# Attention stages of a two-layer model on one core: PV products, copies and routing moved in the order, rotary tables scaled by VectorE

## What is computed

```
xn = layernorm(x)
x  = x + attention8(xn)[pred_values] + moe16(xn)       # 8 heads of 64, causal; 16 experts, 4 chosen
xn = layernorm(x)
x  = x + attention16(xn) + transformer6(xn)            # 16 heads of 8, causal; 6 layers, window 32
# transformer6, in each layer:
q, k = l2norm(q) * q_scale, l2norm(k) * k_scale        # then the rotary product with cos and sin tables
x = attention_window32(...) @ Wo + x ;  x = gelu_ffn(layernorm(x)) + x
```

## Time and profile before

| | us |
|---|---|
| median of 3 runs | 4737.76 |
| lowest, highest | 4735.57, 4738.05 |
| profiled execution, own time | 4733.7 |
| its span | 4731.7 |
| PE busy | 4372.4 (92%) |
| DVE busy | 3262.6 (69%) |
| ACT busy | 2762.9 (58%) |
| POOL busy | 2215.5 (47%) |

### The profile page before, as it was taken

The page is one execution under the profiler, slowest core; times in us unless marked ns, Lnnn a source line. Parts: engine busy times, 40 slices in busy tenths (PEclk is TensorE's granted clock), DMA queues, the critical chain, the costliest instruction groups (busy, mean ns, idle before and its releaser), DMA issues. The chain is left out here.

```text
span 4731.7 us, 170782 instructions
## 1 busy us (share of the span) xinstructions
PE 4372.4 (92%) x67636; PEld 2558.3 (54%) x67636; DVE 3262.6 (69%) x5741; ACT 2762.9 (58%) x5481; POOL 2215.5 (47%) x2020
## 2 busy tenths in 40 slices
PE   7888988898699999999999999999999999999995
PEld 4445544554355555555555555555555555555553
DVE  4556555655377777777777777777777777777772
ACT  4544554455256666666666666666666666566663
POOL 0000000000176676666666666666666666666661
PEclk9999999999899999999999999999999999999997
DMA  1000000000021112211121111211112111221112
GB/s 37 8 6 8 8 3 8 5 8 4 19 63 41 47 46 60 56 44 47 44 65 51 44 48 43 69 48 47 47 54 56 47 47 48 59 51 47 47 47 63
DMA packets 144849, 187.88 MB, mean 40 GB/s; under 512 B 34151, under 2 KB 66298, under 8 KB 144250
## 3 DMA queue, kind: packets, MB, share of 16 engines
q1 hardware_dynamic: 144250, 178.39, 14.0%
HBM read 29.39 MB, written 4.19 MB: 7 GB/s over the span
## 5 line engine op out<-in xcount | busy, mean ns | idle before, releaser
L1343 POOL TENSOR_TENSOR cs<-cs 128x512 f32<-128x512 f32 x768 | 980.5, 1277 | 575.2 <-DVE cs L1654 570.1
L1470 PE MATMUL psum<-wqkv,xw 128*128 128x512 f32 x2304 | 1191.6, 609 | 31.3 <-POOL xw L1380 24.9
L1654 DVE TENSOR_TENSOR cs<-psum,rots 128x1024 f32<-128x1024 f32 x768 | 938.0, 1222 | 295.3 <-PE psum L1470 249.5
L1352 POOL TENSOR_TENSOR qk<-cs,rn 128x512 f32<-128x512 f32 x768 | 777.2, 1044 | 338.0 <-ACT rn L1536 282.6
L1552 ACT ACTIVATE sq<-psum 128x512 f32<-128x512 f32 x768 | 459.2, 598 | 654.0 <-DVE cs L1654 645.3
L1378 POOL MEMSET qTl<- 128x2048 f32 x1 | 1.8, 1805 | 1270.0 <-POOLq L498 1270.0
L1615 DVE TENSOR_REDUCE ss<-sq 128x8 f32<-128x512 f32 x768 | 519.9, 677 | 6.9
L1421 PEld LDWEIGHTS psum<-pT,vw 64*64 64x64 f32 x18624 | 400.0, 135 | 191.1 <-issue 190.9
L1475 PEld LDWEIGHTS psum<-ident,qk 128*128 128x128 f32 x3088 | 352.5, 141 | 265.9 <-issue 152.0
L1475 PE MATMUL psum<-ident,qk 128*128 128x128 f32 x3088 | 445.6, 278 | 49.0 <-DVE state L1688 31.5
L1470 PEld LDWEIGHTS psum<-wqkv,xw 128*128 128x128 f32 x2304 | 368.6, 190 | 195.2 <-issue 169.9
(11 more groups left out here) (205 smaller groups left out, 6927.4 us busy)
## 6 DMA issues: line engine op xcount, KB each, us to landing
vw<-vl SPq DMA_DIRECT2D x768, 128.0 KB, 2.4
vw<-vl SPq DMA_DIRECT2D x672, 64.0 KB, 2.0
wqkv<-in_wqkv SPq DMA_DIRECT2D x42, 256.0 KB, 4.0
wol<-in_wol SPq DMA_DIRECT2D x7, 512.0 KB, 4.0
w1l<-in_w1l SPq DMA_DIRECT2D x7, 341.0 KB
xin<-in_x SPq DMA_DIRECT2D x9, 256.0 KB, 2.9
xr<-in_x SPq DMA_DIRECT2D x8, 256.0 KB, 2.8
sums<-sumout SPq DMA_DIRECT2D x8, 256.0 KB, 2.3
```

The costliest lines, as they stand in the source:

```text
L1343: summed_rot.done(nc.gpsimd.tensor_tensor(own, own, halves(cs[:, t % 2, j, 1, :])[:, :, ::-1, :], ALU.add), at)
L1352: rotated.done(nc.gpsimd.tensor_tensor(qk[:, j, :].rearrange("p (h c) -> p h c", c=EL), cs[:, t % 2, j, 0, :].rearrange("p (h c) -> p h c" ...
L1470: last = nc.tensor.matmul(ps[:, :], xw[:, t * P:(t + 1) * P], wqkv[:, col:col + BANK], start=True, stop=True)
L1654: parts.done(V.tensor_tensor(cs[:, t % 2, j, :, :].rearrange("p i (h c) -> p i h c", c=EL), twice, by_head, ALU.mult), at)
```

## The change

1. `wide_heads`: `at` of unit n-2 now stands ahead of `as` of unit n. PE's transposes come ahead of the scores and DVE's copies ahead of the maxima.
2. `narrow_heads`: the first scores of the next rank come ahead of `bn`, the last two PV products and `oe` of a rank (`rest_of`) come behind the first scores of the next rank (of the last rank: behind `as.0`), and `bp.r.1` comes ahead of `bt.r.2`.
3. Routing: `gr` comes earlier; pieces 0 to 6 stand among the projections, pieces 7 to 12 behind every second unit of the wide heads. `h1.0` comes ahead of the last `ap`.
4. In the second stage DVE scales the rotary tables: once ahead of the loop, and then behind the last `qk` step of each layer's last sample. ACT, DVE and POOL have the 8 samples written out, as PE has.

```diff
 def wide_heads(extra):
     for n in range(UNITS0 + PV_LAG0):
+        if n - TURN_LAG0 in range(UNITS0):
+            out.append(("at", n - TURN_LAG0))
         if n < UNITS0:
             out.append(("as", n))
-        if n - TURN_LAG0 in range(UNITS0):
-            out.append(("at", n - TURN_LAG0))
...
-def narrow_heads(r, scores):
-    s = scores + [[]] * (T - 1 - len(scores))
-    return (s[0] + [("bt", r, 0)] + s[1] + [("bt", r, 1), ("bp", r, 0)] + s[2]
-            + [("bt", r, 2), ("bp", r, 1), ("bp", r, 2), ("bp", r, 3), ("oe", r)])
+def narrow_heads():
+    out = []
+    for r in range(RANKS):
+        first, second, third = [[("bs", r + 1, i)] if r + 1 < RANKS else [] for i in reversed(range(1, T))]
+        out += first
+        out += [("bn", 0)] if r == 0 else rest_of(r - 1)
+        out += [("bt", r, 0)] + second + [("bt", r, 1), ("bp", r, 0)] + third + [("bp", r, 1), ("bt", r, 2)]
+        out += [("bo", r - 1)] if r else []
+        out += [("bn", r + 1)] if r + 1 < RANKS else []
+    return out
+
+def rest_of(r):
+    return [("bp", r, 2), ("bp", r, 3), ("oe", r)]
...
-SPLIT = {n + 1: [("rt", n)] for n in range(ROUTE)}
+EARLY = 7
+SPLIT = {2 * n + 2: [("rt", EARLY + n)] for n in range(ROUTE - EARLY)}
+CLOSE = {UNITS0 + 1: [("h1", 0)]}
...
+LOOP = (PROJECTED[:2] + [("ln",)] + PROJECTED[2:4] + [("gr",)] + PROJECTED[4:5] + [("x1t",), ("rt", 0), ("rt", 1)] + PROJECTED[5:7]
+        + [("rt", 2), ("rt", 3), ("q1",), ("k1",), ("rt", 4)] + PROJECTED[7:8] + [("rt", 5), ("rt", 6), ("v1",)] + PROJECTED[8:9]
+        + [("bs", 0, 3)] + PROJECTED[9:10] + [("bs", 0, 2)] + PROJECTED[10:11] + [("bs", 0, 1)] + PROJECTED[11:] + narrow_heads()
+        + wide_heads({**SPLIT, **CLOSE, 0: rest_of(LAST_RANK), 1: [("bo", LAST_RANK)], 3: [("ot",)], 5: [("y1",)]}) + EXPERT)
...
             with pool.Fori(0, DEPTH) as l:
-                parts.wait_before(pool, l * B, pieces[-1])
-                for a in range(2):
-                    for b in (2 * a, 2 * a + 1):
-                        nc.gpsimd.tensor_tensor(
-                            rots[:, b, :, :], rot[:, b, :, :],
-                            qks[:, a, bass.ds(l, 1), :].to_broadcast([P, T, EL]), ALU.mult).then_inc(scaled, 1)
-                with pool.Fori(0, B) as s:
+                for s in range(B):
...
+            def scale_tables(l):
+                for a in range(2):
+                    for b in (2 * a, 2 * a + 1):
+                        V.tensor_tensor(rots[:, b, :, :], rot[:, b, :, :], qks[:, a, bass.ds(l, 1), :].to_broadcast([P, T, EL]),
+                                        ALU.mult).then_inc(scaled, 1)
...
+            dve.wait_ge(rot_loaded, 48)
+            scale_tables(0)
             with dve.Fori(0, DEPTH) as l:
-                with dve.Fori(0, B) as s:
+                for s in range(B):
                     it = l * B + s
-                    dve.wait_ge(scaled, l * 4 + 8)
+                    dve.wait_ge(scaled, l * 4 + 4)
                     for key in order:
                         read(it, l, s, key)
+                        if s == B - 1 and key == ("qk", *pieces[-1]):
+                            parts.wait(dve, it, pieces[-1])
+                            settle(dve, passed)
+                            scale_tables((l + 1) % DEPTH)
```

More of the change, by code:

```diff
@@ L278 @@
 QUAD = 4
-SPLIT = {n + 1: [("rt", n)] for n in range(ROUTE)}
-EXPERT = ([("gs",), ("h1", 0), ("h3", 0), ("h1", 1), ("ag",), ("h3", 1), ("cq", 0), ("g", 0), ("ab",), ("h1", 2), ("g", 1),
+EARLY = 7
+SPLIT = {2 * n + 2: [("rt", EARLY + n)] for n in range(ROUTE - EARLY)}
+CLOSE = {UNITS0 + 1: [("h1", 0)]}
+EXPERT = ([("gs",), ("h3", 0), ("h1", 1), ("ag",), ("h3", 1), ("cq", 0), ("g", 0), ("ab",), ("h1", 2), ("g", 1),
            ("h3", 2), ("cq", 1)] + expert_chunks(range(3, CH0 + 1))
@@ L284 @@
 FIRST = [("nx", 0), ("nx", 1), ("nx", 2), ("xt",), ("tt",)]
[L285 to L291, removed]
+HEAD = [("gr",)] + projections() + [("rt", n) for n in range(EARLY)] + wide_heads({**SPLIT, **CLOSE}) + EXPERT
+LAST_RANK = RANKS - 1
+LAST = ([("ln",), ("x1t",), ("q1",), ("k1",), ("v1",)] + flat(scores_of(0)) + narrow_heads() + rest_of(LAST_RANK)
+        + [("bo", LAST_RANK), ("ot",), ("y1",)])
 PROJECTED = projections()
[L293 to L296, removed]
+LOOP = (PROJECTED[:2] + [("ln",)] + PROJECTED[2:4] + [("gr",)] + PROJECTED[4:5] + [("x1t",), ("rt", 0), ("rt", 1)] + PROJECTED[5:7]
+        + [("rt", 2), ("rt", 3), ("q1",), ("k1",), ("rt", 4)] + PROJECTED[7:8] + [("rt", 5), ("rt", 6), ("v1",)] + PROJECTED[8:9]
+        + [("bs", 0, 3)] + PROJECTED[9:10] + [("bs", 0, 2)] + PROJECTED[10:11] + [("bs", 0, 1)] + PROJECTED[11:] + narrow_heads()
+        + wide_heads({**SPLIT, **CLOSE, 0: rest_of(LAST_RANK), 1: [("bo", LAST_RANK)], 3: [("ot",)], 5: [("y1",)]}) + EXPERT)
 class Buffers0:
@@ L1334, in _ @@
                 s.prime(pool)
-            pool.sem_inc(scaled, 4)
             def work(it, s, key):
@@ L1380, in _ @@
             nc.gpsimd.tensor_copy(xw[:, :], state[:, 0, :]).then_inc(fetched.sem, 1)
-            pool.wait_ge(rot_loaded, 48)
             with pool.Fori(0, DEPTH) as l:
-                parts.wait_before(pool, l * B, pieces[-1])
-                for a in range(2):
-                    for b in (2 * a, 2 * a + 1):
-                        nc.gpsimd.tensor_tensor(
-                            rots[:, b, :, :], rot[:, b, :, :],
-                            qks[:, a, bass.ds(l, 1), :].to_broadcast([P, T, EL]), ALU.mult).then_inc(scaled, 1)
-                with pool.Fori(0, B) as s:
+                for s in range(B):
                     it = l * B + s
@@ L1591, in _ @@
             with act.Fori(0, DEPTH) as l:
-                with act.Fori(0, B) as s:
+                for s in range(B):
                     it = l * B + s
```

## The result

| | before | after |
|---|---|---|
| median (us) | 4736.66 (4 runs) | 4676.28 (4 runs) |
| lowest, highest | 4734.0, 4738.05 | 4671.95, 4679.21 |
| profiled execution: own time, span | 4733.7, 4731.7 | 4679.21, 4677.4 |
| PE busy | 4372.4 (92%) | 4385.6 (94%) |
| mean length of a LOOP trip | 154.2 | 151.3 |

The ratio is 0.9879, with a 95% interval of 0.9866 to 0.9891: 60 us less in the medians, 54 in the spans. Predicted were 50 (4688 us). The total lies near, the parts do not: the first stage gave 23.4 (predicted 43), the second 31 (predicted 7). One part came 20 short and the other 24 over, from causes that have nothing to do with each other; that the total came near is luck. The trips are read from one residual addition of DVE to the next, the samples from one `xm` to the next; the means are over 7 trips, 5 samples over a border and 42 others.

What follows compares the result with a forecast made beforehand. PE, busy 92% of the span, was taken as the bound, so its idle time could be won. First stage 43 plus second stage 7 made 50 off 4733.7; with 4.1 for the median, about 4688 us, range 4662 to 4714.

Steps and rivals of the forecast that it cites:

- Narrow heads, ranks: First stage, ranks of the narrow heads: the new order saves PE waits of net 4.7 us a trip.
- Front: Front of a first-stage trip: `bt.0.0` comes 1.2 us later, with bounds 0 and 3.
- Wide heads: First stage, wide heads: the new order saves 1.8 us of PE's waits a trip, and 1.8 in sample 0.
- LAST: Last narrow attention: 4 us of the ranks' 4.7 saved, an estimate.
- Second stage, samples: Second-stage samples away from the borders: no saving; a change of more than 0.1 us would show the prediction wrong.
- Borders: Second-stage layer borders: DVE's branch to first product 4.1 us instead of 5.62, saving 1.5 a border, 7.5 in all.
- Tables: Second stage, four tables on DVE in 1.5 us: costs 1 over six layers; tables 0.84 later if DVE waits for POOL.
- (c): Rival, wide heads: transposes wait for exponentials, the 50 us are gone, 4738 us, no change; chance 0.06.
- (e): Rival, narrow heads: the order brings the ranks half of 4.7, 18 us less gain, 4706 us; chance 0.14.
- (d): Rival, second stage: ACT, DVE and POOL fetch written-out code every sample; slower, 4850 us at the full 3.4; chance 0.05.
- (b): Rival, trip's front: routing and maxima fully exposed on DVE, 2.6 + 1.85 a trip instead of 1.2, 4711 us; chance 0.15.
- (a): Rival, second-stage borders: DVE's jump back stays short, saving 14.4 us for 7.5, 4681 us; chance 0.12.

Runs made afterwards that it cites:

- e5: The changed kernel with bn.0 ahead of bs.1.3 again, as before the change; 4652.9 us, ratio 0.9835.
- c1: The kernel before with bn.0 behind bs.1.3 in LOOP and LAST and nothing else changed; 4768.24 us, ratio 1.0070.
- w1: The changed kernel with the wide heads' order of before (scores, transposes, PV products); 4697.88 us, ratio 0.9924.
- u2: The kernel before with the 8 samples written out on DVE, ACT and POOL, tables still on POOL; 4703.94 us, ratio 0.9941.
- e2: The kernel before with the second-stage parts alone (tables on DVE, samples written out); 4690.14 us, ratio 0.9910.
- u1: The kernel before with the 8 samples written out in DVE's program alone, tables still on POOL; 4707.07 us, ratio 0.9947.

## Why the prediction was right in its sum and not in its parts

*Narrow heads, ranks* (4.7 of idle time a trip): right. From the first turned scores to `as.0` PE's waits fell from 11.14 to 5.75, 5.4, or 5.0 with the 0.42 of the last PV products behind `as.0`. The waits of 0.61 and 0.57 stayed in ranks 1 and 2, as said (0.61 and 0.42 in rank 0), and those of 0.71 and 0.48 went.

*Front* (1.2 later): right in idle time, 3.23 to 4.57, and the wait of "about 2.5" ahead of `bt.0.0` was 2.81. The step that failed is what I left out of it. I priced this wait by its length alone, though the longest waits with a clock of 1.00 behind them were 1.51 in the trip and 1.7 at the borders, and the same trace has a low clock from 119.4 to 122.8, at a wait of 2.23. It cost 2.46 of busy time more, in seven trips 17. That is the largest part of what the first stage lacks against 43, and `e5` and `c1` show it.

*Wide heads* (1.8): waits fell from 2.65 to the 0.42 just named, the 0.99 among those that went, more than said, and `w1` puts the order at 1.9 a trip beside the other parts. But against the kernel before, 1.3 of busy time came with it, which I had not looked for, since I counted PE's products as equal in any order. That is also HEAD: 2.1 of waits gone, 1.3 more at the mask, 0.45 more at the transposes, and from `as.0` to the experts 43.43 for 43.38. Predicted was 1.8.

*LAST* (4): 3.5 between the two profiled executions (113.36 and 109.84 from the last residual addition to the second stage's first product), but that this is the order's is not shown. With LAST as before the change it took 113.38 in `u2`, but 109.63 in `e2` and 109.71 in `u1`: in the two long ones (before and `u2`) the clock was low for 23.9 us at one stretch there, in the two short ones for 13.7. With the changed LAST it took 108.6 to 109.8 in five traces. That the number came out near 4 is chance.

*Second stage, samples* (nothing, "if samples away from the borders change by more than 0.1 us"): wrong. They fell by 0.68, 42 of them 29 us of the stage's 31.7; the borders gave 5 x 0.35, its start the rest. The step that failed: "the written-out code is taken as free". I asked what it could cost and not what the loop had cost. The register instructions of `xm`'s line stood in the trace of before, and so did PE's wait on `xm` (`u1`: 0.62 of the 0.68).

*Borders* (7.5, and tables +1): I took 4.1 from DVE's branch to its first product; measured 3.2 to 4.3, with 2.9 to 3.9 for the jump, so its size was right. The rule of the Trainium skill (Runtime: NRT & Kernel Launch, section Instruction fetch mechanics) on taken branches is borne out here by these 2.9 to 3.9, where the same branch over one sample's code had 0.25 behind it. DVE's branch record itself stays at 0.055 to 0.072 (I had said "3.4 or more" of it); the time passes ahead of the next instruction. That should have saved 1.3 to 2.4 a border. In the changed kernel the sample over a border fell by 0.35 only, less than the others. What failed is that one fetch was taken to be all: the second gap of 1.0 to 1.4 took most of the gain, and with it PE's wait for kT reached 2.7 to 3.2 at three borders, behind which the clock fell; those three samples take 73.1 in the mean, against 72.86 before. Without it (`e2`) a border gives 3.0, and against `u2`, with the same samples, 3.1: all of PE's 2.9 of waits.

*Tables*: a group of four takes 2.13, not 1.5. In the six groups in the layers the first table lasts 1.12 to 1.13, the others 0.41, and it ends 0.3 behind POOL's addition, which had begun 0.43 ahead of it. The row over all of them:

```profile
L1622 DVE TENSOR_TENSOR rots<-rot,qks x28: 410/413/1131, 1285.9 to 4573.2; 128x256 f32<-128x256 f32 x28
```

and POOL at the same place:

```profile
1822.26 1.27 POOL L1351 TENSOR_TENSOR cs<-cs 128x512 f32<-128x512 f32 x1 [0.44 <-DVE cs L1661]
```

So my upper bound applied, 0.7 later for 0.84. The Trainium skill (SBUF — State Buffer, section SBUF: two separate sides) states the lock; the trace now agrees, six times over. What it cost PE was not tested apart.

Of the signs, a trip took 150.3 and not 148, the waits for kT were 1.6 to 3.2 and not under 1, and the samples away from the borders changed by 0.68, which was named as a sign of being wrong. Rivals (c) and (e) did not come, nor did (d): no sample got longer. The mechanism of (b), routing and maxima fully exposed, did not come either, but its price nearly did: the front cost 1.3 of waiting and 2.5 by the clock, 3.8 a trip where (b) had 4.45. (a), the whole border gain, did come where the code stood well, though with a long jump.

## What to carry to other kernels

Price a wait of the tensor engine by what it does to the clock as well: here one wait of 2.8 us cost nearly as much again as it was long, and putting the short addition that others wait for ahead of four long maxima gave 3.4 a trip, of which only 0.9 was waiting. Where a loop index is used to find an address, look at the register instructions right ahead of the operation that others wait for; writing the loops out took 29 us of the second stage away, 27 of them by DVE's alone. A written-out loop must still jump back, and what the jump costs depends on where the code lies: if the first operations behind it show a second gap, move the code by a few instructions.

## What the runs showed that I had not expected

- The place of a loop in DVE's program, moved by 8 instructions without any work, decides over a gap of 1.0 to 1.5 us behind each jump back.
- Register arithmetic with a loop's index took 0.3 us in one instruction and held the operation behind it up by 0.5, and it lies in no engine's busy time.
- The granted clock fell to 0.50 behind waits of 2.81 and 3.30 us, not behind 1.51, and stayed there for 6.8 or 10.2 us under products that followed closely, in different trips of one kernel. Waits of PE at a layer border threw it as well, for 3.4 to 6.8 us: each of 2.7 and more, and some of 1.8 to 2.4.
- The last narrow attention took 109.7 or 113.4 us in one and the same order, with the clock.
- A bf16 mask product of 2 x 128 columns is followed by a transpose after 0.12 us and by a PV product after 0.22.
- The first of four small products on DVE lasted 1.13 instead of 0.41 beside an addition on POOL.
